# A linear attention layer with an int8 layer: x supplied transposed for the projections, and the running state updated head by head

## The chip, the cores and the metric

The kernel runs on 1 core of one Trainium2 chip. The number that counts is the device time of one launch in microseconds (us); less is better. An engine is named by its short form in the profile: PE (TensorE, matmuls), PEld (its weight loads), DVE (VectorE), ACT (ScalarE), POOL (GpSimd) and SP (SyncE, which here only issues transfers).

## The reference

Input x has the shape (8, 1024, 512), eight sequences of 1024 rows. There are 16 heads of 32 columns.

```python
x = x + attn(layernorm(x)); x = x + ffn(layernorm(x))      # layernorm: (x - mean) / sqrt(var + 1e-5)

def attn(x, qkv_w, qkv_b, out_w, out_b):
    q, k, v = split(x @ qkv_w.T + qkv_b)                    # (b, head, l, 32) each
    q = relu(q) + 1e-6;  k = relu(k) + 1e-6
    kv = cumsum(einsum('bhld,bhle->bhlde', k, v), axis=2)   # causal sum of k v^T
    k_cum = cumsum(k, axis=2)
    num = einsum('bhld,bhlde->bhle', q, kv)
    den = maximum(einsum('bhld,bhld->bhl', q, k_cum), 1e-6)
    return (num / den) @ out_w.T + out_b

def ffn(x, weight_int8, weight_scale, bias):
    x_scale = maximum(abs(x).max() / 127, 1e-5)             # one maximum over all of x
    x_int8 = clip(round(x / x_scale), -128, 127)
    return (x_int8 @ weight_int8.T) * x_scale * weight_scale.T + bias
```

The maximum over all rows splits the work in two: no row of the second layer can be scaled before the last row of the first is done.

## The kernel before

**Tiles and stages.** The rows are cut into N = 64 chunks of 128 (CB = 8 to a sequence), and two chunks are a group. The first stage (the attention) goes through the chunks in order; the second (the int8 layer) runs over 64 tiles after it. Nearly every product is made of three in float16: a value is split into a high and a low half, and high by high, high by low and low by high are added up in PSUM.

**What a chunk costs in the first stage.** DVE takes the mean and variance of its rows from xs (ln_moments), POOL refines 1/sqrt (refine_rstd), DVE writes the normalised rows xn (ln_normalise, L1578), PE turns them by four products with a float32 identity (transpose_x, L720), ACT and DVE split what comes out of PSUM into xt_hi and xt_lo (split_x, L1145 and L1589). From these PE makes q and k of a group with 8 units of 12 products (project_qk, L737) and v of a chunk with 12 (project_v, L750). The halves of q and k are moved by SP into stack, so that one product with 96 rows gives a head's scores (scores, L786); ACT copies the high half of the scores (L1201), DVE makes the low half (L1612), POOL masks both (mask, L523 and L525). PE multiplies them with v in outputs (L849 to L854), and adds the product of q with the state of all chunks before (L840). POOL also adds the bias of the output to xs (L484) and makes the low halves of q and k (L506) and of v (L515).

**The state.** A head's state is a 32 by 33 matrix (32 columns of v and a column of ones for the denominator). The keys are turned (transpose_keys, L770), and keys_values (L874) multiplies 128 key columns, which are four heads, by the 132 columns of the same four heads of v. Of the 128 by 132 result only the four blocks on the diagonal belong to a head; the rest is worked out and thrown away. For four such sets of heads in three terms that is 12 products, in two calls of six, since 4 times 132 numbers don't fit into one bank of PSUM. DVE adds each half to state (L1732), POOL multiplies state by a mask of ones and zeros (mask_state, L539), ACT and POOL split that into s_hi and s_lo (L546). The last chunk of a sequence has no update, so there are 56.

**Order.** Each engine has its own list of calls, written out by hand: a start, a loop body of one group, and an end. An engine works strictly in the order of its list, and semaphores tie the lists together. UNITS is the order in which the results of transpose_x, transpose_keys, project_qk and project_v take turns in the two banks of unit.

## Time and profile before

| | us |
|---|---|
| median of 3 runs | 1075.56 (1075.49 to 1076.29) |
| the profiled execution: its time | 1075.05 |
| the profiled execution: its span in the trace | 1073.3 |
| PE busy | 1047.6 (98%) |
| POOL busy | 866.1 (81%) |
| DVE busy | 806.8 (75%) |
| ACT busy | 727.8 (68%) |

The span runs from the first to the last instruction in the trace; the time of the execution is 1.75 us longer. "Busy" is the time in which at least one instruction of that engine was running. A matmul's duration runs until its last result is out, while the next one starts long before, so what a matmul costs PE in a dense stretch is the distance from its start to the next start and not its duration. The cost of an instruction on another engine is its duration.

### The profile page before, as it was taken

Reading aid. Unit: us, or ns where it says so; the run is one execution under the profiler, and the core shown is the slowest. Engines: PE = TensorE matmul, PEld = TensorE weight load, DVE = VectorE, ACT = ScalarE, POOL = GpSimd, SP = SyncE. Lnnn points to the kernel's source line nnn. Section 1 sums busy time; section 2 is a strip of 40 time slices with the busy share of each in tenths; the row PEclk is TensorE's granted clock in tenths of the full one; section 3 lists DMA queues with packets and bytes.
Section 4 is the critical chain, followed back from the end, with each engine's and each line's share of the span. In section 5 each row is a group of like instructions: output and inputs, shape, how many; then the busy total and the mean of one; then the engine's idle time right before and its main releaser. Section 6 shows DMA issues by size and latency. Waiting matters only on the chain.

```text
span 1073.3 us, 29299 instructions
## 1 busy us (share of the span) xinstructions
PE 1047.6 (98%) x10735; PEld 779.6 (73%) x10735; DVE 806.8 (75%) x1603; ACT 727.8 (68%) x1319; POOL 866.1 (81%) x1094
## 2 busy tenths in 40 slices
PE   5999999999999999999999999999999999998998
PEld 3777777778778777777787877877777777764554
DVE  5867777778787778777777777777777777698776
ACT  6776666676676666666766766666667667654997
POOL 2579887878788888888788887888788888893998
PEclk9999999999999999999999999999999999999999
DMA  7323343333333333333333333333333333233995
GB/s 274 80 50 93 97 109 94 86 81 91 92 90 90 86 92 97 100 88 88 91 87 87 88 92 90 87 100 99 90 87 81 90 91 93 51 117 103 383 403 211
DMA packets 74976, 120.69 MB, mean 112 GB/s; under 512 B 16465, under 2 KB 16977, under 8 KB 74834
## 3 DMA queue, kind: packets, MB, share of 16 engines
q1 hardware_dynamic: 74304, 118.29, 37.6%
q8 instruction: 86, 1.41, 0.6%
q10 hardware_dynamic: 530, 0.54, 0.2%
q14 instruction: 56, 0.46, 0.1%
HBM read 36.97 MB, written 31.46 MB: 64 GB/s over the span
## 4 chain that ended last, share of the span: by engine, by line
PE 93%; DVE 3%; ACT 1%; issue 1%; DMA 1%; POOL 1%; SPq 0%; DVEq 0%; ACTq 0%; POOLq 0%
PE unit L737 30%; PE unit L750 15%; PE misc L818 14%; PE acc L2188 5%; PE sc L786 5%; PE o_st L874 4%; PE o_st L840 3%; PE o_st L849 3%; PE unit L720 3%; PE misc L804 2%; PE unit L770 2%; PE o_st L854 2%; PE tp L2178 1%; PE acc L2193 1%; DMA stack<-qkv_wt 1%
## 5 line engine op out<-in xcount | busy, mean ns | idle before, releaser
L737 PE MATMUL unit<-xt_hi,w_hi 128*128 128x256 f16 x1000 | 273.0, 273 | 2.4 <-ACT relu L1159 2.2
L737 PE MATMUL unit<-xt_hi,w_lo 128*128 128x256 f16 x1000 | 272.9, 273 | 0.0
L737 PE MATMUL unit<-xt_lo,w_hi 128*128 128x256 f16 x1000 | 272.9, 273 | 0.0
L1159 ACT ACTIVATE relu<-unit,qk_bias_scaled 128x256 f32<-128x256 f32 x250 | 117.5, 471 | 152.1 <-PE unit L737 151.6
L1612 DVE SCALAR_TENSOR_TENSOR x_ring<-sc,x_ring 128x512 f16<-128x512 f32 x256 | 174.3, 684 | 46.8 <-ACT x_ring L1201 44.0
L506 POOL TENSOR_TENSOR qk_lo<-f_t,qk_hi 128x512 f16<-128x512 f32 x128 | 148.4, 1160 | 56.1 <-ACT qk_hi L1178 56.1
L1201 ACT ACTIVATE x_ring<-sc 128x512 f16<-128x512 f32 x256 | 148.0, 591 | 59.0 <-PE sc L786 59.0
L523 POOL TENSOR_SCALAR_AFFINE_SELECT x_ring<-x_ring 128x512 f16<-128x512 f16 x256 | 164.3, 642 | 26.4 <-DVE x_ring L1612 26.1
L525 POOL TENSOR_SCALAR_AFFINE_SELECT x_ring<-x_ring 128x512 f16<-128x512 f16 x256 | 168.0, 656 | 0.0
L737 PEld LDWEIGHTS unit<-xt_hi,w_hi 128*128 128x128 f16 x1000 | 97.8, 98 | 20.7 <-ACT relu L1159 3.0
L737 PEld LDWEIGHTS unit<-xt_lo,w_hi 128*128 128x128 f16 x1000 | 97.9, 98 | 16.4
L737 PEld LDWEIGHTS unit<-xt_hi,w_lo 128*128 128x128 f16 x1000 | 97.9, 98 | 11.6
L539 POOL TENSOR_TENSOR s_own<-state,own_head 128x528 f32<-128x528 f32 x56 | 75.2, 1343 | 28.3 <-DVE state L1732 17.5
L750 PE MATMUL unit<-w_hi,xt_hi 128*128 128x512 f16 x256 | 97.1, 379 | 0.0
L750 PE MATMUL unit<-w_hi,xt_lo 128*128 128x512 f16 x256 | 96.9, 379 | 0.0
L750 PE MATMUL unit<-w_lo,xt_hi 128*128 128x512 f16 x256 | 96.9, 379 | 0.0
L818 PE MATMUL misc<-wo_hi,at_hi 128*128 128x512 f16 x248 | 94.0, 379 | 1.6 <-DVE at_lo L1620 1.5
L786 PE MATMUL sc<-stack 96*128 96x128 f16 x1024 | 93.5, 219 | 0.8 <-DVE x_ring L1612 0.7
L818 PE MATMUL misc<-wo_hi,at_lo 128*128 128x512 f16 x248 | 94.0, 379 | 0.0
L818 PE MATMUL misc<-wo_lo,at_hi 128*128 128x512 f16 x248 | 94.0, 379 | 0.0
L1177 ACT ACTIVATE f_t<-relu,eps_scaled 128x512 f32<-128x512 f32 x128 | 92.0, 719 | 0.9 <-PE o_st L854 0.4
L546 POOL TENSOR_TENSOR s_lo<-s_own,s_hi 128x528 f16<-128x528 f32 x56 | 69.8, 1246 | 27.4 <-ACT s_hi L1222 27.4
(224 smaller groups left out, 2711.0 us busy)
## 6 DMA issues: line engine op xcount, KB each, us to landing
stack<-qk_hi SPq DMA_DIRECT2D x504, 64.0 KB, 2.0
xs<-x SPq DMA_DIRECT2D x64, 256.0 KB, 2.7
stack<-qk_lo SPq DMA_DIRECT2D x256, 64.0 KB, 2.0
out<-res SPq DMA_DIRECT2D x64, 256.0 KB, 5.3
x_spill<-xs SPq DMA_DIRECT2D x56, 256.0 KB, 2.3
x_ring<-x_spill SPq DMA_DIRECT2D x56, 256.0 KB, 5.6
stack<-qkv_wt SPq DMA_DIRECT2D x6, 512.0 KB, 8.2
x_ring<-out_wt SPq DMA_DIRECT2D x1, 1024.0 KB, 12.1
```

The lines of the kernel that those rows point to most:

```text
L506: pool.tensor_tensor(qk_lo[:, g % 2, own, :], f_t[:, own, :], qk_hi[:, g % 2, own, :], ALU.subtract).then_inc(qk_lo_done, 1)
L523: pool.affine_select(out=am_hi[:, c % 2, r, :, :], in_=am_hi[:, c % 2, r, :, :], compare_op=ALU.is_ge, fill=0.0, base=0, pattern=[[0, HG], ...
L525: pool.affine_select(out=am_lo[:, c % 2, r, :, :], in_=am_lo[:, c % 2, r, :, :], compare_op=ALU.is_ge, fill=0.0, base=0, pattern=[[0, HG], ...
L539: pool.tensor_tensor(s_own[:, :, :, :], state[:, :, :, :], own_head[:, :, :, :], ALU.mult).then_inc(s_masked, 1)
L737: mm = pe.matmul(dst[:, 0:GT], wp[:, k, f:f + P], xp[:, g % 2, k, :], start=(n == 0), stop=(n == len(terms) - 1))
L750: mm = pe.matmul(dst, xp[:, g % 2, k, j * P:(j + 1) * P], wp[:, k, 2 * E:3 * E], start=(n == 0), stop=(n == len(terms) - 1))
L786: mm = pe.matmul(sc[:, r % 2, n, :], stack[0:3 * D, par, 0, h, at], stack[0:3 * D, par, 1, h, at], start=True, stop=True)
L818: mm = pe.matmul(out_bank(c), xp[:, k, :], wp[:, k, :], start=(n == 0), stop=(n == len(terms) - 1))
L1159: act.activation(relu[:, i % 4, :], src[:, 0:GT], ACT.Relu, bias=qk_bias_scaled[:, f:f + 1]).then_inc(qk_done, 1)
L1177: act.activation(f_t[:, own, :], relu[:, at, :], ACT.Identity, bias=eps_scaled[:, side:side + 1]).then_inc(qk_eps_done, 1)
L1201: act.activation(am_hi[:, c % 2, r, :, :], sc[:, r % 2, :, :], ACT.Copy, scale=SCORE_FACTOR).then_inc(sc_copied, 1)
L1612: dve.scalar_tensor_tensor(out=am_lo[:, c % 2, r, :, :], in0=sc[:, r % 2, :, :], scalar=SCORE_FACTOR, in1=am_hi[:, c % 2, r, :, :], op0=AL ...
```

## The change

Three things change, and the lists of all engines are written anew for them.

**x supplied turned.** The kernel gets x a second time, with rows and columns of each sequence swapped (x_turned). For the chunks from 4 on, PE no longer turns anything: SP loads a group of turned rows into x_tr (load_turned). The mean and 1/sqrt of a row are now needed along the free dimension and on every partition, so they are written to memory (store_ln, 512 single numbers) and read back spread over all partitions (spread_ln) into ln_of. DVE subtracts the one and multiplies by the other in place (centre_x and scale_x), then ACT and DVE split as before, with the source in SBUF instead of PSUM. The statistics are taken from a further copy of the rows, xa (load_rows), up to eight groups ahead, so x is read three times. The first four chunks go the old way.

**The state head by head.** keys_values is one call of 32 products. A product takes the 32 key columns of one head and writes to the 32 partitions of PSUM that are this head's. With the high half of the keys it multiplies the high and the low half of v at once, 66 columns, and with the low half of the keys the high half of v, 33 columns. state shrinks from 528 to 264 numbers on a partition, in two parts that POOL adds (s_sum) ahead of the mask. DVE adds to state once per chunk and not twice.

**Buffers and semaphores.** x_tr and xa take the place at the start of x1_ring where weights were staged; the staging of out_wt goes to xs, and the last four of the first eight chunks are loaded into xs later. Semaphores are merged.

```diff
-wo_stage = spare[:, 0:EC * E].rearrange("p (c n) -> p c n", c=EC)
+x_tr = spare[:, 0:4 * E].rearrange("p (s k t) -> p s k t", s=2, k=EC)
+xa = spare[:, 4 * E:8 * E].rearrange("p (s c e) -> p s c e", s=2, c=GROUP)
+wo_stage = xs[:, AHEAD:CB, :]
...
-state = buf(one, "state", [P, HG, 4, VW])
-own_head = buf(one, "own_head", [P, HG, 4, VW])
+state = buf(one, "state", [P, HG, 2, VW])
+s_sum = buf(one, "s_sum", [P, HG, VW])
+own_head = buf(one, "own_head", [P, 4, VW])
...
-UNITS = (("v", 1), ("xt", 1), ("kt", 1), ("qk", 0), ("qk", 1),
-         ("qk", 2), ("qk", 3), ("qk", 4), ("qk", 5), ("qk", 6),
-         ("kt", 0), ("qk", 7), ("xt", 0), ("v", 0))
+UNITS = (("kt", 1), ("v", 1), ("qk", 3), ("qk", 4), ("kt", 0),
+         ("qk", 5), ("qk", 6), ("qk", 7), ("v", 0), ("qk", 0),
+         ("qk", 1), ("qk", 2))
...
+    def load_rows(g, since=3):
+        if not since <= g < N // GROUP:
+            return
+        if g >= 4:
+            sp.wait_ge(ln_stats, upto(GROUP * (g - 2) + 1))
+        if g == 2:
+            sp.wait_ge(bias_squared, 1)
+            sp.wait_ge(sums_ready, 3)
+        sp.dma_start(xa[:, g % 2, :, :], x_pairs[g]).then_inc(xa_loaded[g % 2], 16)
+    def load_turned(g, since=3):
+        if not since <= g < N // GROUP:
+            return
+        if g >= 4:
+            sp.wait_ge(xt_lo_done, upto(GROUP * (g - 2) + 1))
+        sp.dma_start(x_tr[:, g % 2, :, :], x_turned_of[g]).then_inc(turned_loaded[g % 2], 16)
...
+    def store_ln(g, since=3):
+        if not since <= g < N // GROUP:
+            return
+        sp.wait_ge(ln_step, (g + 1) * LN_STEPS)
+        sp.dma_start(ln_rows[g].rearrange("k c p -> p (k c)"), mrv[:, g % 2, 0:2, :].rearrange("p k c -> p (k c)"),
+                     allow_slow_non_contiguous=True).then_inc(ln_stored[g % 2], 16)
+    def spread_ln(g, since=3):
+        if not since <= g < N // GROUP:
+            return
+        sp.wait_ge(ln_stored[g % 2], g // 2 * 16)
+        if g >= 4:
+            sp.wait_ge(xt_ready, upto(GROUP * (g - 2) + 1))
+        sp.dma_start(ln_of[:, g % 2, :, :].rearrange("p k t -> p (k t)"),
+                     ln_rows[g].rearrange("k c p -> (k c p)").partition_broadcast(P)).then_inc(turned_loaded[g % 2], 16)
...
-    for n in range(6, N - 2, GROUP):
+    for n in range(8, N - 2, GROUP):
         g = n // GROUP
+        load_rows(g + 8)
+        store_x1(n - 5)
+        load_next_x(n - 8)
...
-        pool.wait_ge(s_added, 2 * updates(c) + 2)
+        pool.wait_ge(s_added, updates(c) + 1)
         if updates(c) > 0:
             pool.wait_ge(s_lo_done, updates(c))
-        pool.tensor_tensor(s_own[:, :, :, :], state[:, :, :, :], own_head[:, :, :, :], ALU.mult).then_inc(s_masked, 1)
+        pool.tensor_tensor(s_sum[:, :, :], state[:, :, 0, :], state[:, :, 1, :], ALU.add).then_inc(s_summed, 1)
+        pool.wait_ge(s_summed, updates(c) + 1)
+        pool.tensor_tensor(s_own[:, :, :, :], s_sum[:, :, :].unsqueeze(2).to_broadcast([P, HG, 4, VW]), own_head[:, :, :].unsqueeze(1).to_broadcast([P, HG, 4, VW]), ALU.mult).then_inc(s_masked, 1)
...
-    def keys_values(c, half):
+    def keys_values(c):
         if not updates_state(c):
             return
         par, _at = place(c)
-        if half == 0:
-            pe.wait_ge(kn_done, updates(c) + 1)
-            pe.wait_ge(v_lo_done, upto(c))
-        if 2 * updates(c) + half > 0:
-            pe.wait_ge(s_added, 2 * updates(c) + half)
-        terms = ((0, v_hi), (0, v_lo), (1, v_hi))
-        for i in range(2):
-            g = 2 * half + i
-            for n, (kp, vp) in enumerate(terms):
-                mm = pe.matmul(st[:, i * 4 * VW:(i + 1) * 4 * VW].rearrange("p (h w) -> p h w", w=VW), kn[:, kp, g, :],
-                               vp[:, par, c % GROUP, 4 * g:4 * g + 4, :],
-                               start=(i == 0 and n == 0), stop=(i == 1 and n == len(terms) - 1), skip_group_check=True)
+        pe.wait_ge(kn_done, updates(c) + 1)
+        pe.wait_ge(v_lo_done, upto(c))
+        if updates(c) > 0:
+            pe.wait_ge(s_added, updates(c))
+        for g in range(HG):
+            for a in range(4):
+                pe.matmul(st[a * D:(a + 1) * D, 2 * g * VW:2 * (g + 1) * VW].rearrange("p (s w) -> p s w", w=VW),
+                          kn[:, 0, g, a * D:(a + 1) * D], v_halves[:, par, c % GROUP, 4 * g + a, :, :],
+                          start=(g == 0), stop=False, skip_group_check=True)
+            for a in range(4):
+                mm = pe.matmul(st[a * D:(a + 1) * D, (2 * g + 1) * VW:2 * (g + 1) * VW], kn[:, 1, g, a * D:(a + 1) * D],
+                               v_hi[:, par, c % GROUP, 4 * g + a, :], start=False, stop=(g == HG - 1), skip_group_check=True)
...
-        project_v(g, 1)
-        transpose_attn(n - 3)
-        scores(n - 1, 2)
-        keys_values(n - 2, 1)
...
+        outputs(n, 1)
+        transpose_keys(n + 1)
+        scores(n + 1, 3)
+        project_v(g + 2, 1)
+        scores(n + 2, 0)
+        project_out(n - 1)
+        project_qk(g + 2, 3)
+        keys_values(n + 1)
...
-        if src is None:
-            src = unit[:, unit_bank[("xt", c % GROUP)], :]
-        if c >= AHEAD:
+        if c < AHEAD:
+            src = (unit[:, unit_bank[("xt", c % GROUP)], :] if src is None else src).rearrange("p (c n) -> p c n", c=EC)
+        else:
+            src = x_tr[:, c // GROUP % 2, :, c % GROUP * P:(c % GROUP + 1) * P]
             act.wait_ge(qk_ready, (c // GROUP - 1) * QK)
             act.wait_ge(v_ready, upto(GROUP * (c // GROUP) - 3))
         act.wait_ge(xt_ready, upto(c))
         act.activation(xt_hi[:, c // GROUP % 2, :, c % GROUP * P:(c % GROUP + 1) * P],
-                       src.rearrange("p (c n) -> p c n", c=EC), ACT.Copy).then_inc(xt_hi_done, 1)
+                       src, ACT.Copy).then_inc(xt_hi_done, 1)
...
+        if g >= 4:
+            dve.wait_ge(ln_stored[g % 2], (g - 2) // 2 * 16)
+        if g >= 2:
+            dve.wait_ge(xa_loaded[g % 2], g // 2 * 16)
         for c in (GROUP * g, GROUP * g + 1):
-            dve.wait_ge(x_loaded[c % CB], (c // CB + 1) * 16)
-            dve.bn_stats(stats[:, c % GROUP, :], xs[:, c % CB, :]).then_inc(ln_stats, 1)
+            if g < 2:
+                dve.wait_ge(x_loaded[c], 16)
+            rows = xs[:, c, :] if g < 2 else xa[:, g % 2, c % GROUP, :]
+            dve.bn_stats(stats[:, c % GROUP, :], rows).then_inc(ln_stats, 1)
         for c in (GROUP * g, GROUP * g + 1):
             dve.wait_ge(ln_stats, upto(c))
             dve.nop(nofuse=True)
-            dve.bn_aggr(mv[:, c % GROUP, :], stats[:, c % GROUP, :]).then_inc(ln_mv, 1)
+            dve.bn_aggr(mrv[:, g % 2, 0:3:2, c % GROUP], stats[:, c % GROUP, :]).then_inc(ln_mv, 1)
         dve.wait_ge(ln_mv, upto(GROUP * g + 1))
-        dve.tensor_scalar(ve[:, :], mv[:, :, 1], LN_EPS, None, ALU.add).then_inc(ln_var, 1)
+        dve.tensor_scalar(ve[:, :], mrv[:, g % 2, 2, :], LN_EPS, None, ALU.add).then_inc(ln_var, 1)
...
+    def turned(c):
+        return x_tr[:, c // GROUP % 2, :, c % GROUP * P:(c % GROUP + 1) * P]
+    def spread(c, kind):
+        return ln_of[:, c // GROUP % 2, kind, c % GROUP * P:(c % GROUP + 1) * P].unsqueeze(1).to_broadcast([P, EC, P])
+    def centre_x(c, since=AHEAD):
+        if not since <= c < N:
+            return
+        g = c // GROUP
+        dve.wait_ge(turned_loaded[g % 2], g // 2 * 32)
+        dve.tensor_tensor(turned(c), turned(c), spread(c, 0), ALU.subtract).then_inc(x_centred, 1)
+    def scale_x(c, since=AHEAD):
+        if not since <= c < N:
+            return
+        dve.wait_ge(x_centred, upto(c - AHEAD))
+        dve.tensor_tensor(turned(c), turned(c), spread(c, 1), ALU.mult).then_inc(xt_ready, 1)
...
-    def add_to_state(c, half):
+    def add_to_state(c):
         if not updates_state(c):
             return
-        dve.wait_ge(st_ready, 2 * updates(c) + half + 1)
+        dve.wait_ge(st_ready, updates(c) + 1)
         if updates(c) > 0:
             dve.wait_ge(s_masked, updates(c))
-        own = state[:, 2 * half:2 * half + 2, :, :].rearrange("p g h w -> p (g h w)")
-        new = st[:, 0:8 * VW]
+        own = state[:, :, :, :].rearrange("p g s w -> p (g s w)")
+        new = st[:, 0:2 * HG * VW]
...
+        "x_turned": np.swapaxes(L0_attn_x, 1, 2),
```

In the loop of PE, transpose_x is gone and keys_values stands once. What the names mean: L720 turns a chunk, L874 updates half of the state, L786 are scores, L737 and L750 are projections. In the middle of the program PE had this order:

```order
L737 MATMUL unit<-xt_hi,w_lo 128x256
L720 MATMUL unit<-ident,xn 128x128 x4
L874 MATMUL o_st<-v_halves,kn 128x132 x6
L786 MATMUL sc<-stack 128x128 x4
L750 MATMUL unit<-w_hi,xt_hi 128x512
```

In the changed kernel the place of an update, between two projections, reads:

```order
L834 MATMUL unit<-xt_hi,w_lo 128x256
L971 MATMUL o_st<-v_halves,kn 32x66 x4
L975 MATMUL o_st<-v_halves,kn 32x33 x4
L971 MATMUL o_st<-v_halves,kn 32x66 x4
L975 MATMUL o_st<-v_halves,kn 32x33 x4
L971 MATMUL o_st<-v_halves,kn 32x66 x4
L975 MATMUL o_st<-v_halves,kn 32x33 x4
L971 MATMUL o_st<-v_halves,kn 32x66 x4
L975 MATMUL o_st<-v_halves,kn 32x33 x4
L850 MATMUL unit<-w_hi,xt_hi 128x512
```

The four turning products are gone, and two times six products of 132 columns have become 16 of 66 and 16 of 33.

On DVE, the statistics (L1553), the normalising (L1578) and the low half of xt (L1589) of a group stood like this in the loop, with L1612 the low half of scores and L1705 to L1716 the division:

```order
L1553 BN_STATS stats<-xs 128x6 x2
L1557 BN_AGGR mv<-stats 128x2 x2
L1559 TENSOR_SCALAR ve<-mv 128x2
L1612 SCALAR_TENSOR_TENSOR x_ring<-sc,x_ring 128x512
L1566 RECIPROCAL r<-sq 128x2
L1578 TENSOR_SCALAR xn<-xs,mv,rstd 128x512 x2
L1612 SCALAR_TENSOR_TENSOR x_ring<-sc,x_ring 128x512
L1705 TENSOR_SCALAR den<-o_st,den_eps 128x16
L1708 RECIPROCAL rden<-den 128x16
L1710 TENSOR_TENSOR o_st<-o_st,num 128x2x7x32
L1716 TENSOR_TENSOR attn<-o_st,rden 128x512
L1589 TENSOR_TENSOR xt_lo<-unit,xt_hi 128x4x128
```

In the changed kernel L1707 subtracts the mean (x_ring with ln_of is x_tr), L1714 scales, L1749 is the low half of scores, L1740 adds the bias of v and L1842 to L1853 are the division:

```order
L1749 SCALAR_TENSOR_TENSOR x_ring<-sc,x_ring 128x512
L1707 TENSOR_TENSOR x_ring<-x_ring,ln_of 128x4x128
L1757 TENSOR_TENSOR at_lo<-misc,at_hi 128x512
L1749 SCALAR_TENSOR_TENSOR x_ring<-sc,x_ring 128x512
L1842 TENSOR_SCALAR den<-o_st,den_eps 128x16
L1845 RECIPROCAL rden<-den 128x16
L1847 TENSOR_TENSOR o_st<-o_st,num 128x2x7x32
L1853 TENSOR_TENSOR attn<-o_st,rden 128x512
L1740 TENSOR_TENSOR v<-unit,v_bias 128x16x32
L1714 TENSOR_TENSOR x_ring<-x_ring,ln_of 128x4x128 x2
L1749 SCALAR_TENSOR_TENSOR x_ring<-sc,x_ring 128x512
```

Where a chunk had one instruction with one tile as its source, it now has two, each with two sources in SBUF, and the scaling of both chunks of a group stands in a row.

## Rows read from the trace of the kernel before

**Rows 1.** The page: busy time and share of the span, by engine.
```profile
PE 1047.6 (98%) x10735; PEld 779.6 (73%) x10735; DVE 806.8 (75%) x1603; ACT 727.8 (68%) x1319; POOL 866.1 (81%) x1094
```
**Rows 2.** Windows: length, busy us per engine with instructions, clock, DMA share, GB/s.
```profile
core 0: us, PE busy (x) PEld busy (x) DVE busy (x) ACT busy (x) POOL busy (x), PEclk, DMA share, GB/s
0.00:60.00 60.00, 46.81 (x364) 32.46 (x365) 41.73 (x87) 42.29 (x71) 26.96 (x48) 0.97 0.53 169
...
100.00:935.00 835.00, 834.93 (x8951) 644.67 (x8948) 631.72 (x1232) 556.62 (x1038) 688.77 (x893) 1.00 0.33 89
...
1000.00:1073.00 73.00, 69.09 (x474) 37.05 (x472) 51.66 (x106) 66.44 (x103) 68.58 (x54) 1.00 0.88 329
```
**Rows 3.** Windows for line L804 alone, four products per chunk, same stretch.
```profile
100.00:935.00 835.00, 33.80 (x224) 25.70 (x224) 1.00 0.33 89
```
**Rows 4.** Waits of PE: who waited for whom, us in total, times, longest.
```profile
PE o_st L885 <- ACT x_ring L1266: 12.0, 2, 9.0
PE unit L818 <- DVE at_lo L1620: 2.5, 2, 1.4
PE unit L737 <- ACT relu L1159: 2.2, 2, 1.5
```
**Rows 5.** Timeline of PE: start us, duration us, then the instruction.
```profile
502.26 0.53 PE L874 MATMUL o_st<-v_halves,kn 128*128 128x132 f16 x6
502.62 0.60 PE L720 MATMUL unit<-ident,xn 128*128 128x128 f32 x4
503.06 0.39 PE L786 MATMUL sc<-stack 96*128 96x128 f16 x4
...
503.64 0.19 PE L849 MATMUL o_st<-v_halves,x_ring 128*128 128x66 f16 x1
503.67 0.18 PE L854 MATMUL o_st<-v_halves,x_ring 128*128 128x33 f16 x1
503.69 0.19 PE L849 MATMUL o_st<-v_halves,x_ring 128*128 128x66 f16 x1
503.73 0.18 PE L854 MATMUL o_st<-v_halves,x_ring 128*128 128x33 f16 x1
503.75 0.19 PE L849 MATMUL o_st<-v_halves,x_ring 128*128 128x66 f16 x1
```
**Rows 6.** Groups of DVE instructions: busy us, mean ns, idle before and its releaser.
```profile
L1578 DVE TENSOR_SCALAR xn<-xs,mv,rstd 128x512 f32<-128x512 f32 x64 | 50.5, 828 | 34.7 <-POOL rstd L498 34.7
L1589 DVE TENSOR_TENSOR xt_lo<-unit,xt_hi 128x512 f16<-128x512 f32 x62 | 42.2, 682 | 6.9 <-ACT xt_hi L1145 6.9
L1732 DVE SCALAR_TENSOR_TENSOR state<-o_st,state 128x264 f32<-128x264 f32 x96 | 41.0, 427 | 18.3 <-PE o_st L874 17.7 <-POOL s_own L539 0.5
L1837 DVE TENSOR_SCALAR x_ring<-w_safe 128x512 f32<-128x512 f32 x1 | 0.4, 417 | 0.0
L1839 DVE TENSOR_TENSOR w_safe<-w_safe,x_ring 128x512 f32<-128x512 f32 x1 | 0.7, 681 | 0.0
```
**Rows 7.** Groups of POOL instructions.
```profile
L539 POOL TENSOR_TENSOR s_own<-state,own_head 128x528 f32<-128x528 f32 x56 | 75.2, 1343 | 28.3 <-DVE state L1732 17.5 <-DVE state L1730 10.9
L493 POOL TENSOR_TENSOR t<-t,ve 128x2 f32<-128x2 f32 x32 | 6.3, 196 | 2.5
```
**Rows 8.** Line L539: duration ns min/median/max, first and last start.
```profile
L539 POOL TENSOR_TENSOR s_own<-state,own_head x56: 1298/1307/3281, 60.7 to 960.9; 128x528 f32<-128x528 f32 x56
```
**Rows 9.** Timeline of DVE, two stretches.
```profile
60.43 2.34 DVE L1825 SCALAR_TENSOR_TENSOR wo_lo<-x_ring,wo_scale,wo_hi 128x2048 f16<-128x2048 f32 x1
...
492.84 1.60 DVE L1578 TENSOR_SCALAR xn<-xs,mv,rstd 128x512 f32<-128x512 f32 x2 [1.22 <-POOL rstd L498]
```
**Rows 10.** Timeline of POOL, the same two stretches.
```profile
60.66 3.28 POOL L539 TENSOR_TENSOR s_own<-state,own_head 128x528 f32<-128x528 f32 x1 [0.71 <-DVE state L1730]
...
492.75 0.64 POOL L523 TENSOR_SCALAR_AFFINE_SELECT x_ring<-x_ring 128x512 f16<-128x512 f16 x1
493.34 0.81 POOL L525 TENSOR_SCALAR_AFFINE_SELECT x_ring<-x_ring 128x512 f16<-128x512 f16 x1
```
**Rows 11.** The page: DMA queue, packets, MB, share of 16 engines' span.
```profile
q1 hardware_dynamic: 74304, 118.29, 37.6%
```
**Rows 12.** The page: DMA issues, KB each, median us from issue to landing.
```profile
xs<-x SPq DMA_DIRECT2D x64, 256.0 KB, 2.7
```

More of the change, by code:

```diff
@@ new lines, in _ @@
+                scores(5, 3)
+                outputs(4, 1)
+                keys_values(5)
+                project_out(3)
+                project_v(4, 1)
+                project_qk(4, 3)
+                scores(6, 0)
+                scores(6, 1)
+                outputs(5, 0)
+                outputs(5, 1)
+                transpose_attn(4)
+                scores(6, 2)
+                project_qk(4, 4)
+                transpose_keys(6)
+                project_qk(4, 5)
+                project_out(4)
@@ new lines, in _ @@
+                project_qk(4, 6)
+                project_qk(4, 7)
+                project_v(5, 0)
+                scores(6, 3)
+                keys_values(6)
+                scores(7, 0)
+                project_qk(5, 0)
+                outputs(6, 0)
+                scores(7, 1)
+                transpose_attn(5)
+                project_qk(5, 1)
+                project_qk(5, 2)
+                scores(7, 2)
+                outputs(6, 1)
+                project_v(5, 1)
+                project_out(5)
@@ new lines, in _ @@
+                scores(7, 3)
+                scores(8, 0)
+                project_qk(5, 3)
+                project_qk(5, 4)
+                scores(8, 1)
+                transpose_attn(6)
+                outputs(7, 0)
+                outputs(7, 1)
+                scores(8, 2)
+                project_out(6)
+                scores(8, 3)
+                transpose_keys(8)
+                project_qk(5, 5)
+                project_qk(5, 6)
+                project_qk(5, 7)
+                project_v(6, 0)
@@ L1440, in _ @@
+                ln_root(7)
                 split_attn(3)
[L1442 to L1455 removed]
+                features(4, 0)
@@ L1456, in _ @@
+                features(5, 0)
+                features(5, 1)
+                features(5, 2)
+                copy_low(6)
+                copy_scores(7, 2)
+                copy_scores(7, 3)
+                split_state(6)
+                split_x(12)
+                split_x(13)
+                copy_scores(8, 0)
+                split_values(9)
+                for n in range(8, N - 2, GROUP):
+                    g = n // GROUP
                     copy_scores(n, 1)
                     split_attn(n - 2)
+                    features(g + 1, 3)
+                    split_values(n + 2)
```

1112 lines of the change are left out of this document (557 added, 555 removed).

## Prediction

> **What bounds the kernel now.** I read four views, from coarse to fine. The page's first part shows PE busy for 98% of the span and POOL next with 81% [rows 1]. That average mixes stages, so the windows come second: from 100 to 935 us PE is busy 834.93 of 835 us, POOL 688.77, DVE 631.72 and ACT 556.62, at full clock [rows 2]. PE works on four turning products of L804 per chunk, and there are 224 in the window [rows 3], so it holds 56 chunks and a chunk lasts 835 / 56 = 14.91 us. Third, the waits of PE: after the 12 us for squares of the weights at the start, its two longest sums are 2.5 and 2.2 us [rows 4]. So in the first stage the time is the sum of what PE is given to do, and nothing else is late. In the last 73 us ACT and POOL are busy for 66 and 69 us and the DMA engines for 88% [rows 2]; the second stage is not touched. Work taken from PE in the first stage is a gain until another engine becomes the bound: per chunk POOL has 14.91 - 688.77 / 56 = 14.91 - 12.30 = 2.61 us to spare, DVE 3.63, ACT 4.97.
>
> **The turning products go.** The fourth view is PE's timeline. Four products of L720 start at 502.62 us and the next line at 503.06 [rows 5]: 0.44 us a chunk. 60 of the 64 chunks lose them, 60 x 0.44 = 26.4 us, and since no time of PE is idle there, all of it lies on the path. What replaces them runs on SP, DVE and ACT. ACT does what it did.
>
> **The state update on PE.** Six products of 132 columns take 502.62 - 502.26 = 0.36 us [rows 5], so a chunk's two calls take 0.72. The trace has no product that uses part of the array's columns, so I bound it. A pair of 66 and 33 columns takes (503.75 - 503.64) / 2 = 0.055 us in outputs [rows 5]. If the 16 pairs of a chunk go one behind another, 16 x 0.055 = 0.88 us. If the four products that write to four different strips of partitions run side by side, 4 x 0.055 = 0.22 us. If besides PE has to empty before the first and after the last of them, there is the part of a product that others now cover: L854 lasts 0.18 us and the next starts 0.03 later, so 0.15 us twice, and 0.88 + 0.30 = 1.18 us. I take 0.75, near the row of single pairs, with a little overlap: +0.03 x 56 = +1.7 us. The ends are -0.50 x 56 = -28 and +0.46 x 56 = +26 us.
>
> The Trainium skill ("TensorEngine Tiling (Array Packing)", Key Properties) says that tiles of the array can load weights and multiply in parallel, and that a change of tiling mode drains the engine. The first would give about the -28 end, the second the drain of the +26 end; no row here shows either, since every product of before has 128 columns of weights.
>
> **DVE.** A chunk loses the normalising, 0.83 us, and one of two additions to the state, 0.43 x 7/8 = 0.37 [rows 6]. It gains centre_x and scale_x: 512 float32 numbers from two tiles in SBUF took 0.68 us at L1839 [rows 6], so 1.36 us. split_x keeps its 0.68. The sum is 11.28 + 1.36 - 1.20 = 11.44 us of about 14.5, and fits.
>
> **POOL.** The new addition has 132 columns; between 0.20 us for 2 columns [rows 7] and 1.31 for 528 [rows 8] it comes to 0.20 + 130 / 526 x 1.11 = 0.47 us, or 0.41 per chunk. The multiplication keeps its 528 columns. That alone gives 12.71 us.
>
> But POOL and DVE hold each other up, and this is the term to weigh. L1825 reads two tiles in SBUF from 60.43 to 62.77 us [rows 9]; L539 starts on POOL at 60.66 and takes 3.28 us [rows 10] where its median is 1.31 [rows 8]. It loses 1.97 us and so stands still until 62.63, 0.14 before DVE is done. An instruction of 0.68 us with two sources in SBUF thus costs a POOL that has work up to 0.54 us. The other way round, L1578 takes 0.83 us on average beside a busy POOL and the same kind 0.42 without one (L1837) [rows 6], and the select that comes up during it takes 0.81 instead of 0.64 [rows 9, 10]. The change makes three DVE instructions per chunk of this sort: centre_x, scale_x, and split_x, whose source moves from PSUM to SBUF. It takes away one L1578. POOL: 12.71 + 3 x 0.54 - 0.17 = 14.16 us per chunk. DVE: 0.4 us of waiting for each of the three, as L1578 had, 11.44 + 1.2 = 12.6.
>
> The Trainium skill ("SBUF — State Buffer", Who interferes with whom) states that a VectorE instruction with two SBUF inputs contends with a GpSimd instruction that reads SBUF, and that the second to issue fully blocks. Rows 9 and 10 agree for the case in which DVE is first, POOL loses 1.97 of the 2.11 us from its start to DVE's end; that DVE waits with two plain sources when POOL is first, no row of before shows.
>
> PE would now need 14.91 - 0.44 + 0.03 x 7/8 = 14.50 us per chunk, POOL 14.16. The room of POOL falls from 2.61 to 0.34 us. Both keep their lists' order, so a delayed select or qk_lo will now and then reach PE through scores or outputs. I charge 4 us for the stage, 0.07 per chunk, between nothing and the rival below.
>
> **Transfers.** Each group of two chunks adds 512 single numbers, 512 packets of x_turned, 256 of rows and 128 of the spread, 1408 packets. A packet took 0.376 x 16 x 1073.3 / 74304 = 0.087 us of one engine [rows 11], so 1408 x 0.087 / 16 = 7.7 us in 29, 26% on top of the 33% of the stage [rows 2]. These are four DMAs more per group in SP's queue, between stack transfers. But SP's loop issues the rows for the statistics (g + 8) one group, 29 us, before DVE's loop reads them (g + 7), and the turned rows and the spread (g + 4) two groups before centre_x (g + 2). A load of 256 KB lands in 2.7 us [rows 12]. PE waits for no DMA now. I charge nothing; if the cover were gone, each group would pay up to 2.7 us.
>
> **Start and end.** The first 60 us hold 13 us of idle PE [rows 2], nearly all for the squares [rows 4]. The lists there are reordered, with three sums of squares ahead of the first projection instead of two. I take 0, with 3 us either way.
>
> **Sum.** 1075.05 - 26.4 + 1.7 + 4 = 1054.4 for an execution like the profiled one. That one was 0.5 us under the median of the runs, so I forecast 1055 us, its own range 1045 to 1066.
>
> **Rivals.** *The strips run side by side.* For it: four products in a row go to four different strips. PE would then need 14.91 - 0.44 - 0.44 = 14.03 us and POOL's 14.16 is the bound; with 0.2 us of idle it gives 14.36, and 56 x 0.55 = 31 us less, 1044; if POOL is held up less than I think, down to 1075.6 - 26.4 - 28 = 1021. I put the case at 1038.
>
> *Each update empties the array twice.* 1075.6 - 26.4 + 26 = 1075, plus up to 4 us of waits: 1075 to 1079, no gain. For it: 0.15 us of every small product is now hidden by the next. Against it: the order puts each update between long projections, whose weights are loaded ahead.
>
> *POOL becomes the bound: slower than before.* Of POOL's 2.61 us of idle time per chunk, part is waiting for ACT and DVE, which its work does not shorten. If half of it, 1.3 us, stays on top of 14.16, a chunk takes 15.46 and the stage 0.55 x 56 = 31 us more, 1106. It decides from 14.91 - 14.16 = 0.75 us of idle POOL per chunk. For it: rows 9 and 10, and that the two scalings and the two splits stand in pairs, between which POOL can take the port again. Against it: much of that idle time is there because PE is slow today.
>
> *The numbers of LayerNorm come late.* The mean and 1/sqrt go out as single numbers and back over all partitions, and SP waits for each step in its own order, with stack transfers behind. If that wait took the place of the products removed, the gain of 26 us would be eaten: 1080 or more. Against it: SP stores group g + 6, spreads g + 4 and DVE centres g + 2 in the same turn of the loop, so each step has two groups, 58 us.
>
> **How the numbers follow.** Forecast 0.42; strips side by side 0.22; array emptied 0.14; POOL as the bound 0.18; LayerNorm late 0.04. A change under 0.2%, 2.2 us, can't be told from none. Faster: 0.42 + 0.22 + 0.05 of the third = 0.69. Same: 0.05 of the third. Slower: 0.04 of the third, 0.18 and 0.04 = 0.26. The range runs from 1032, which holds most of the second case, to 1084, which holds the third and leaves out most of the fourth.
>
> **What will show it.** The windows from 100 to 900 us with 56 chunks: a period near 14.6, PE still above 97% busy, POOL above 93%. In PE's timeline, 32 products of the update within 0.75 us: 0.25 would mean side by side, 1.2 with gaps at both ends the emptying. centre_x and scale_x at 0.68 us alone and about 1.1 on average, and POOL's selects at L615 more often above 0.64. The waits of PE with sums of several us on DVE's low scores or POOL's masks. The forecast is wrong if PE's waits sum to over 15 us, or if a DMA stands in them.

## The result and the profile after

The kernel after takes 1105.07 us (median of 3 runs, 1104.89 to 1110.37) against 1075.56: a ratio of 1.029, 95% interval 1.024 to 1.034. It is slower; 1055 was forecast. Its profiled execution was the longest of the three, 1110.37 us. Its trace spans 1108.6 us, 35.3 more than before, so what follows accounts for these 35.3 us and not for the 29.5 between the medians.

The page's first lines (busy us by engine, then PE's clock in tenths over 40 slices and the DMA queue), against [rows 1] and [rows 11]:

```profile
PE 1030.3 (93%) x11615; PEld 731.3 (66%) x11615; DVE 856.0 (77%) x1607; ACT 727.7 (66%) x1319; POOL 922.1 (83%) x1150
...
PEclk9999898999999999999999999999999999979999
...
q1 hardware_dynamic: 118464, 157.68, 50.3%
```

PE is busy for 17 us less and stands still for 53 us more. The windows say where (the columns of [rows 2]; the last one answers to its third):

```profile
0.00:60.00 60.00, 40.42 (x222) 23.64 (x223) 34.15 (x78) 33.09 (x54) 21.45 (x41) 0.94 0.61 189
60.00:200.00 140.00, 114.17 (x1294) 82.95 (x1293) 88.09 (x165) 72.17 (x139) 99.83 (x135) 0.93 0.55 112
200.00:930.00 730.00, 714.82 (x8654) 527.33 (x8652) 602.43 (x1085) 495.68 (x920) 650.90 (x820) 1.00 0.48 132
1035.00:1108.00 73.00, 69.34 (x475) 37.17 (x473) 51.73 (x107) 66.69 (x103) 68.76 (x54) 1.00 0.88 331
```

From 200 us on PE is busy for 98%; before that it stands still for 45 of 200 us, and the clock falls to 0.93. The kernel before has, behind its first window [rows 2],

```profile
60.00:200.00 140.00, 138.33 (x1493) 107.88 (x1491) 101.14 (x198) 95.32 (x177) 118.16 (x152) 1.00 0.32 86
```

and stands still for 15 of the 200 us. To follow the loss I take the start of the last turning product of attention of a chunk, in the traces (for chunk 8 it is the last of these four, before and after):

```profile
186.65 0.61 PE L804 MATMUL misc<-ident,attn 128*128 128x128 f32 x4
```
```profile
233.29 0.61 PE L904 MATMUL misc<-ident,attn 128*128 128x128 f32 x4
```

The table gives how many us later than in the kernel before that start comes, for the kernel after and for the experiments below; the last column is the time from chunk 8 to chunk 58, over 50 (14.85 us before).

```
                            chunk 0     4     8    32    58    63   us per chunk
after                          15.8  41.6  46.6  40.9  26.6  35.2   14.45
e1 state update alone           0.5   0.4  -0.4  -6.3 -13.0 -11.2   14.60
e2 no store                     6.7  14.2  13.3   2.6 -14.4  -6.7   14.30
e3 store on ACT's queue        35.3  56.4  72.9  78.6  84.2  92.4   15.08
e4 one source                  18.7  45.8  51.6  47.5  36.3  45.4   14.54
e5 rows of 32                   9.3  17.4  15.0   3.1 -13.0  -5.7   14.29
e6 128 single numbers          12.8  28.9  28.2  21.2   5.4  13.3   14.40
e7 no store, no loads           7.0  13.9  10.5   0.3 -15.2  -7.6   14.34
e8 no store, one source         6.7  12.5  11.7   0.6 -16.2  -6.6   14.29
e9 no wait at the spread       16.7  39.2  37.5  31.3  18.0  26.0   14.46
e10 stores from group 10 on     6.9  15.0  18.3  10.9  -0.5   7.4   14.47
```

So the 35 us are +46.6 in the first eight chunks, -20.0 in the next fifty and +8.6 in the last five. The steady stretch did what I forecast (14.57 us per chunk), and a little more.

PE's waits after, against [rows 4], where none named a DMA (who waited for whom, us in total, times, longest):

```profile
PE sc L886 <- DMA stack<-qk_lo: 16.6, 3, 6.9
PE sc L886 <- issue: 12.8, 15, 2.1
PE unit L834 <- ACT relu L1253: 9.8, 5, 6.5
PE o_st L985 <- ACT x_ring L1360: 9.0, 3, 8.0
```

and of SP's:

```profile
SPq L391 <- DMA ln_rows<-mrv: 18.4, 4, 6.5
```

The scores now wait for transfers. What SP does at the first such wait, in its timeline:

```profile
37.55 1.86 SPq L447 DMA_DIRECT2D stack<-qk_lo  x3
39.46 0.59 SPq L380 DMA_DIRECT2D ln_rows<-mrv  x1
40.09 0.54 SPq L373 DMA_DIRECT2D x_ring<-x_turned  x1
41.06 2.43 SPq L447 DMA_DIRECT2D stack<-qk_lo  x4
```

and how the chain of waits goes on from there, and at 82 us (start, duration, what):

```profile
42.90 12.17 DMA stack<-qk_lo
55.07 0.14 issue
55.20 1.01 PE sc L886 x8
...
82.27 10.27 DMA ln_rows<-mrv
92.56 0.34 SPq L391
```

A stack transfer lands in 2.0 us at the median. This one took 12.17; the store of LayerNorm's single numbers (L380) had been issued 3.4 us ahead of it, and behind the store a load of turned rows (L373), which e5 below has in the same place. The store of 82.27 took 10.27 us to land, and SP stood at the spread (L391) for the end of it. The waits name the store only at L391; what it does to the transfers behind it shows as their landing.

It does it to transfers of another queue too. ACT issues eight stack transfers of its own (stack<-qk_hi, L1400) from 37.6 us on, in its own queue. Here are the last five of them, issued behind SP's store of 39.46, in the kernel after, and the same five in e5, which stores the same numbers as rows (count, duration of the issue in ns, starts; then us from issue to landing):

```profile
L1400 ACTq DMA_DIRECT2D stack<-qk_hi x5: 546/612/828, 39.7 to 42.5; - x5
DMA to landing us min/median/max: 9.2/11.7/11.8
```
```profile
L1401 ACTq DMA_DIRECT2D stack<-qk_hi x5: 612/617/815, 39.9 to 42.5; - x5
DMA to landing us min/median/max: 2.1/4.1/4.3
```

So the delay is not in SP's queue alone: it lies where the transfers of both queues pass.

### The profile page after: what moved, and what is told of

It reads as the page before. It is cut to its first block, busy times and chain, and to the rows that moved or that the text cites. A ratio compares the mean times of both kernels' runs of the same rounds, so it can differ in the third digit from the quotient of the medians.

```text
span 1108.6 us, 31189 instructions
## 1 busy us (share of the span) xinstructions
PE 1030.3 (93%) x11615; PEld 731.3 (66%) x11615; DVE 856.0 (77%) x1607; ACT 727.7 (66%) x1319; POOL 922.1 (83%) x1150
## 4 chain that ended last, share of the span: by engine, by line
PE 77%; DMA 7%; DVE 6%; issue 3%; ACT 3%; SPq 2%; POOL 1%; another core or an unknown queue 0%; ACTq 0%; DVEq 0%; POOLq 0%
PE unit L834 24%; PE unit L850 13%; PE misc L918 13%; PE sc L886 5%; PE acc L2340 5%; PE o_st L940 3%; DMA ln_rows<-mrv 3%; PE o_st L949 3%; PE misc L904 2%; PE unit L870 2%; SPq L447 2%; PE o_st L954 1%; PE tp L2330 1%; DMA stack<-qk_lo 1%; PE acc L2345 1%
## 5 line engine op out<-in xcount | busy, mean ns | idle before, releaser
L613 POOL TENSOR_SCALAR_AFFINE_SELECT x_ring<-x_ring 128x512 f16<-128x512 f16 x256 | 177.9, 695 | 28.5 <-DVE x_ring L1749 28.2
L1749 DVE SCALAR_TENSOR_TENSOR x_ring<-sc,x_ring 128x512 f16<-128x512 f32 x256 | 172.7, 683 | 27.2 <-ACT x_ring L1295 26.8
L596 POOL TENSOR_TENSOR qk_lo<-f_t,qk_hi 128x512 f16<-128x512 f32 x128 | 152.7, 1207 | 32.7 <-ACT qk_hi L1272 31.8
L615 POOL TENSOR_SCALAR_AFFINE_SELECT x_ring<-x_ring 128x512 f16<-128x512 f16 x256 | 176.1, 688 | 0.0
L886 PE MATMUL sc<-stack 96*128 96x128 f16 x1024 | 94.0, 222 | 37.2 <-DMA stack<-qk_lo 16.6
L886 PEld LDWEIGHTS sc<-stack 96*128 96x128 f16 x1024 | 68.8, 98 | 68.0 <-issue 33.1
L638 POOL TENSOR_TENSOR s_lo<-s_own,s_hi 128x528 f16<-128x528 f32 x56 | 67.5, 1206 | 52.1 <-ACT s_hi L1316 52.1
```

The source lines that it names most:

```text
L596: pool.tensor_tensor(qk_lo[:, g % 2, own, :], f_t[:, own, :], qk_hi[:, g % 2, own, :], ALU.subtract).then_inc(qk_lo_done, 1)
L613: pool.affine_select(out=am_hi[:, c % 2, r, :, :], in_=am_hi[:, c % 2, r, :, :], compare_op=ALU.is_ge, fill=0.0, base=0, pattern=[[0, HG], ...
L615: pool.affine_select(out=am_lo[:, c % 2, r, :, :], in_=am_lo[:, c % 2, r, :, :], compare_op=ALU.is_ge, fill=0.0, base=0, pattern=[[0, HG], ...
L638: pool.tensor_tensor(s_lo[:, c % 2], s_own[:, :, :, :], s_hi[:, c % 2], ALU.subtract).then_inc(s_lo_done, 1)
L886: mm = pe.matmul(sc[:, r % 2, n, :], stack[0:3 * D, par, 0, h, at], stack[0:3 * D, par, 1, h, at], start=True, stop=True)
L1749: dve.scalar_tensor_tensor(out=am_lo[:, c % 2, r, :, :], in0=sc[:, r % 2, :, :], scalar=SCORE_FACTOR, in1=am_hi[:, c % 2, r, :, :], op0=AL ...
```

## The experiments

Twelve kernels ran. The kernel before, timed again beside them, took 1075.96 us (for e1 to e4), 1075.75 (e5 to e8) and 1075.14 (e9 to e12); each ratio is against the one of its own set. "Price" is the time above e2, the kernel without the store.

**e1, the state update alone.** In the kernel before, the six products of 132 columns in each of two calls become 32 products of one head each in one call, with POOL's addition:

```diff
-state = buf(one, "state", [P, HG, 4, VW])
+state = buf(one, "state", [P, HG, 2, VW])
+s_sum = buf(one, "s_sum", [P, HG, VW])
```

> The kernel before with the state update alone taken from the change: 32 products of one head each in one call at the place of the first of the two calls, the halved state, POOL's added sum; x is turned on PE as before, and every list keeps its order. From the changed kernel's trace the 32 products take about 0.3 us against 0.72. If PE stays the bound, 56 x 0.42 = 23.5 us less: about 1052. If the strips cost a wait around each update after all, or POOL's extra 0.4 us per chunk reaches PE, over 1060. If this part is what made the changed kernel slow, over 1076.

1063.51 us, ratio 0.988 (0.987 to 0.990), where 1052 was expected if PE stayed the bound, and over 1060 if the strips cost a wait or POOL's addition reached PE: half of the change is a gain by itself, 12.4 us, and the fastest kernel of all. PE's timeline in the kernel after shows the price (start, duration):

```profile
507.87 0.27 PE L834 MATMUL unit<-xt_hi,w_lo 128*128 128x256 f16 x1
508.07 0.21 PE L971 MATMUL o_st<-v_halves,kn 128*32 128x66 f16 x4
508.11 0.19 PE L975 MATMUL o_st<-v_halves,kn 128*32 128x33 f16 x4
...
508.29 0.19 PE L975 MATMUL o_st<-v_halves,kn 128*32 128x33 f16 x4
508.40 0.39 PE L850 MATMUL unit<-w_hi,xt_hi 128*128 128x512 f16 x1
```

Products of four strips start as one group, and eight groups start within 0.22 us. From 507.87 to 508.40 are 0.53 us, of which the product ahead takes 0.11 itself (the spacing in its series): 0.42 us a chunk, against 0.72 before. Within it the first group comes 0.20 us after the product ahead, 0.09 more than its own 0.11, and the product behind 0.11 after the last group. Between "side by side" (0.22) and "emptied twice" (1.18) it is the first with a part of the second. The gain of 0.30 x 56 = 17 us shrinks to 12.4; what takes the rest no run shows.

**e2, no store.** Of the kernel after, with the waits for it:

```diff
-sp.dma_start(ln_rows[g]..., mrv[:, g % 2, 0:2, :]...)
-sp.wait_ge(ln_stored[g % 2], g // 2 * 16)
-    ln_rows[g].rearrange("k c p -> (k c p)").partition_broadcast(P)
+    out_b.partition_broadcast(P)
```

> The changed kernel without the store of the mean and 1/sqrt as 512 single numbers: SP still waits for the numbers, then spreads a fixed row of the same size (out_b) in place of them, so the rows it normalises with are not the right ones. Queue theory (the store lies 7 to 14 us in SP's one queue with bulk loads ahead and stack transfers behind it, and SP stands at the spread until it has landed): the loss of the first 200 us goes, 1105 - 35 = about 1070, and the steady stretch gets shorter too, down to 1055. Port theory (DVE's instructions with two sources in SBUF and POOL hold each other up): under 8 us less, 1097 to 1105.

1070.78 us, ratio 0.996 (0.994 to 0.997), 34 less than the kernel after. Queue theory holds (about 1070), though nothing of its further gain down to 1055; port theory (1097 to 1105) is out. At chunk 8 it is 13.3 us late instead of 46.6, and it gains 0.55 us per chunk instead of 0.40. One store in 29 us, of 2 KB, is the loss. (e2 also drops the waits for the store; e9 and e5 below separate the two.)

**e3, the store on ACT's queue**, issued behind the next group's square root:

```diff
-sp.dma_start(ln_rows[g]...)
+act.wait_ge(ln_step, (g + 1) * LN_STEPS)
+act.dma_start(ln_rows[g]...)
```

> The changed kernel with that store issued by ACT into its own queue, one group later than before on SP's list, right after the root of the next group; nothing left out. Queue theory: stack transfers no longer lie behind the store, but the spread still waits for it: 1070 to 1090. Port theory: no change, 1100 to 1110.

1168.89 us, ratio 1.087 (1.085 to 1.090). All expectations missed. The store now comes a group later, and DVE waits for what it feeds:

```profile
DVE x_ring L1716 <- DMA ln_of<-ln_rows: 29.5, 2, 17.6
DVE stats L1676 <- DMA ln_rows<-mrv: 12.0, 1, 12.0
```

This run can't tell the queue from what lies behind it, since it moved the store in time too. The landings of ACT's transfers in the section above can.

**e4, one source.** DVE's centring, scaling and low half are left out, and in their place stand instructions that read one source and write one number (the first of three is shown):

```diff
-dve.tensor_tensor(turned(c), turned(c), spread(c, 0), ALU.subtract)
+dve.tensor_reduce(scrap[:, 0, c:c + 1], turned(c), AX.XY, ALU.max)
```

> The changed kernel with DVE's centring, scaling and low half of x replaced (chunks from 4 on) by a maximum over the same tile, which reads one source in SBUF and takes as long alone (0.65 to 0.69 us): what is left out is the normalising of x and its low half. Port theory: DVE's waits of 0.2 to 0.4 us at each and POOL's longer selects go; the steady stretch falls from 14.4 to about 14.1 us per chunk, 56 x 0.3 = 17 us, 1088, and if the start is held up by POOL too, 1075. Queue theory: the start keeps its loss, over 1090.

1119.79 us, ratio 1.040 (1.037 to 1.042), over the 1090 of queue theory and far from port theory's 1088: slower still, though POOL's busy time fell from 922.1 to 870.0 us and DVE's from 856.0 to 812.8. POOL's selects show what they were held up by, 643 ns instead of 688 (busy us, mean ns, idle time ahead):

```profile
L616 POOL TENSOR_SCALAR_AFFINE_SELECT x_ring<-x_ring 128x512 f16<-128x512 f16 x256 | 164.6, 643 | 0.0
```
```profile
L615 POOL TENSOR_SCALAR_AFFINE_SELECT x_ring<-x_ring 128x512 f16<-128x512 f16 x256 | 176.1, 688 | 0.0
```

The contention is real. That it is not what makes the kernel late, e8 shows. Why it got 15 us slower I did not settle.

**e5, rows of 32.** DVE turns the numbers in blocks of 32 x 32 (mrv is widened to 32 columns), and the store writes 16 rows of 128 bytes; the result is that of the kernel after. In the loop the store stands one group later in SP's list (g + 5 instead of g + 6), since the turning comes between:

```diff
+dve.transpose(mrt[:, g % 2, :], mrv[:, g % 2, :, :].rearrange("p k c -> p (k c)"))
-sp.dma_start(ln_rows[g]..., mrv[:, g % 2, 0:2, :]...)
+for q in range(4):
+    sp.dma_start(ln_rows[g].rearrange("k c p -> (k c) p")[:, q * 32:(q + 1) * 32],
+                 mrt[q * 32:q * 32 + 4, g % 2, :])
```

> The kernel after with LayerNorm's numbers stored as rows: DVE turns each block of 32 x 32 numbers (one more small instruction per two chunks), so that the 512 single numbers become 16 rows of 32 numbers, in four DMAs of four rows. Everything else of the change stays, the result too. Theory (the landing of 512 single numbers holds SP's queue and through it the stack transfers and the spread): the store then lands like other small transfers, nothing stands behind it, and the time comes to that of the kernel without the store, 1070.8 us, within 4 us: 1067 to 1075. Rival (what costs is that the numbers go through DRAM and back at all, a write's completion of several us whatever its count of rows): 1095 to 1110.

1071.75 us, ratio 0.997 (0.996 to 0.998): as without a store, and faster than the kernel after by 33 us and than the kernel before by 4. In SP's timeline the same place as above is

```profile
39.57 1.66 SPq L382 DMA_DIRECT2D ln_rows<-mrt  x4
41.28 0.53 SPq L374 DMA_DIRECT2D x_ring<-x_turned  x1
41.86 2.46 SPq L449 DMA_DIRECT2D stack<-qk_lo  x4
```

and PE starts the scores at 53.68 from DVE's work, with no DMA in the chain:

```profile
52.34 0.69 DVE v L1751
53.03 0.61 DVE x_ring L1760
...
53.68 0.40 PE sc L887 x4
```

**e6, 128 single numbers** instead of 512:

```diff
-sp.dma_start(ln_rows[g]..., mrv[:, g % 2, 0:2, :]...)
+sp.dma_start(ln_rows[g, 0, 0], mrv[:, g % 2, 0, 0:1])
```

> The kernel after with a quarter of the store: only the means of the first chunk of a group go out, 128 single numbers instead of 512, and the spread reads one bias vector in their place, so LayerNorm's numbers are wrong; all waits stay. Theory (the price is per single number): between the kernel without the store, 1070.8, and the kernel after, 1105, near a quarter of the way: 1076 to 1085. Rival (a price per store, whatever its size): over 1095.

1090.32 us, ratio 1.015 (1.011 to 1.019): a quarter of the numbers costs more than half of the price. Neither expectation holds as it stands.

**e7, no store and no loads** from group 4 on: load_rows, load_turned and spread_ln return at once there.

> The kernel without the store (1070.8 us), and also without the transfers that replace the turning, from group 4 on: rows for the statistics, turned rows, spread. DVE works on what lies there, so the numbers of x are wrong. Theory A (the bulk loads cost through the queue: the start loses 13 us and the end 8 by stack transfers that stand behind them): the start loss shrinks to 7 or less and the time falls to 1050 to 1060. Theory B (the loss at start and end lies in the order of the lists and in DVE's and POOL's longer instructions): within 3 us of 1070.8.

1066.62 us, ratio 0.991 (0.990 to 0.993). 4 us less: 84 transfers of 256 to 512 KB cost almost nothing. Theory A (1050 to 1060, and 7 us or less lost at the start) is out, since 10.5 us are still lost by chunk 8; theory B's 3 us are missed by 1.2. Most of what is left is not the queue.

**e8, no store and one source**, e2 with the edit of e4:

> The kernel without the store, in which DVE's centring, scaling and low half of x (from chunk 4 on) are replaced by a maximum over the same numbers that reads one source and writes one number, so that DVE holds the port less; the numbers of x are wrong. Theory (what is left of the loss is DVE and POOL holding each other up): below 1065, with the steady stretch gaining about 0.7 us per chunk against the kernel before instead of 0.55. Rival (the port is not on the path): within 3 us of 1070.8.

1067.24 us, ratio 0.992 (0.990 to 0.994). 3.5 us less, between the theory (below 1065) and its rival (within 3 us of 1070.8), and 14.29 us per chunk as in e2 (14.30): the port costs at most 3 or 4 us here. Where, the traces don't show: the profiled executions of e2 and e8 took the same, 1068.32 and 1068.48 us.

**e9, no wait at the spread**, the store stays:

```diff
-sp.wait_ge(ln_stored[g % 2], g // 2 * 16)
```

> The kernel after with the store of 512 single numbers as it is, but SP does not wait for it at the spread, which reads one bias vector instead, so LayerNorm's numbers are wrong; only DVE still waits for a store two groups old before it writes over its source. Theory A (what costs is that SP stands at the spread until the store has landed, with everything behind it in its list): near the kernel without the store, 1070.8 us, at most 1078. Theory B (the store holds up the transfers that are issued behind it, whether SP waits or not): over 1088, and the stack transfers behind a store still take 8 us and more. I hold B, since 10 us went by in the trace between a store's issue and the landing of a load behind it.

1102.18 us, ratio 1.025 (1.023 to 1.026). Theory B (over 1088) holds: SP's standing at the spread is worth 3 us of the 34. (By the table it would be 9, but there the kernel after stands with its longest execution.) The scores wait as before for what was issued behind the store:

```profile
PE sc L885 <- DMA stack<-qk_lo: 16.4, 3, 7.3
```

**e10, stores from group 10 on.**

```diff
-if not since <= g < N // GROUP:
+if not 10 <= g < N // GROUP:
```

> The kernel after with the stores of single numbers from group 10 on only, as in the loop; the first eight are left out, and all spreads read one bias vector, so LayerNorm's numbers are wrong. Theory (in the steady loop the store hides: there after gained 0.4 us per chunk with the store and 0.55 without it; the price is paid in the first eight chunks, where five stores stand among transfers that PE waits for): 1071 plus about 0.15 x 40 = 6 at most, 1071 to 1079. Rival (each store costs about the same anywhere): 22 of 30 stores are left, so 1071 + 34 x 22 / 30 = 1096.

1083.55 us (1077.38 to 1085.42), ratio 1.007 (1.005 to 1.009). Theory (1071 to 1079) and rival (1096) were both missed. 22 of 30 stores cost 12.8 of the 34 us, 0.6 each; the first eight cost 21.5, 2.7 each. The place decides, but the loop doesn't hide them: 14.47 us per chunk against 14.30 without.

**e11, 16 single numbers.**

```diff
-sp.dma_start(ln_rows[g]..., mrv[:, g % 2, 0:2, :]...)
+sp.dma_start(ln_rows[g, 0, 0, 0:16], mrv[0:16, g % 2, 0, 0:1])
```

> The kernel after with a store of 16 single numbers in place of 512, the spread reading one bias vector, so LayerNorm's numbers are wrong; all waits stay. 512 numbers cost 34 us of time, 128 cost 19.5, 16 rows of 128 bytes cost 1. Theory A (the number of single writes sets the price): 1071 to 1074. Theory B (a write of 4 bytes lands late however few there are): 1085 to 1092, as with 128.

1069.93 us, ratio 0.994 (0.993 to 0.996): no price. Theory B (1085 to 1092) is out.

**e12, 128 rows of 4 numbers**, all 512 numbers in 128 writes of 16 bytes:

```diff
-sp.dma_start(ln_rows[g].rearrange("k c p -> p (k c)"), mrv...)
+sp.dma_start(ln_rows[g].rearrange("k c p -> (k c p)").rearrange("(p f) -> p f", f=4), mrv...)
```

> The kernel after with the store as 128 rows of 4 numbers, one for each partition, all 512 numbers in 128 writes of 16 bytes; the spread reads one bias vector, so LayerNorm's numbers are wrong; all waits stay. Theory A (the number of writes sets the price): as the kernel that stores 128 single numbers, 1090, within 4 us. Theory B (the size of a write sets it, and 16 bytes are easier than 4): 1071 to 1082.

1069.06 us, ratio 0.995 (0.994 to 0.997): no price, and theory A (1090) is out. e6 and e12 send the same number of packets; the pages' lines on the queue and on the store (KB each, median us to landing) read, for e6,

```profile
q1 hardware_dynamic: 106944, 157.64, 51.3%
ln_rows<-mrv SPq DMA_DIRECT2D x30, 0.5 KB, 10.2
```

and for e12

```profile
q1 hardware_dynamic: 106944, 157.68, 50.2%
ln_rows<-mrv SPq DMA_DIRECT2D x30, 2.0 KB, 6.5
```

Four times the bytes land 3.7 us sooner and the kernel is 21 us faster. Together:

| store of a group | writes x bytes | us |
|---|---|---|
| none (e2) | | 1070.8 |
| e11 | 16 x 4 | 1069.9 |
| e5 | 16 x 128 | 1071.8 |
| e12 | 128 x 16 | 1069.1 |
| e6 | 128 x 4 | 1090.3 |
| after | 512 x 4 | 1105.1 |

Many writes of 4 bytes are what costs; neither their number alone (e12) nor their size alone (e11). One rival stands untested: e6 puts its 128 numbers side by side in memory, so 16 of its writes fall on 64 bytes where e12 has 4. Whether the size of a write or the crowding of writes on one place sets the price would take a store of 128 single numbers spread apart.

## Why the prediction was wrong

**The step that failed is "Transfers".** I priced the single numbers by the mean packet of the queue, 0.087 us of one engine, and by the room in their due times, and charged nothing. The share itself came out smaller than I worked out: from 200 to 930 us the DMA engines' share is 0.48 for 0.33 before, 0.15 more, where I had 0.26. A single number takes far less of it than a mean packet: by the pages of the kernel after and of e12, which stores as many bytes in a quarter of the writes, 11520 packets more go with 348 us more, 0.03 us each and not 0.087. So the price was not in the share. 512 writes of 4 bytes landed after 10.27 us, and transfers issued behind them, whose due times were not two groups off, landed with them: the stack transfers, which PE waits for. I had looked at how early LayerNorm's numbers were stored and not at who stands behind them in SP's list at the start. e2, e5 and e9 show it: 34 us come back without the store, 33 with the store as rows, and only 3 without SP's wait.

The rival *The numbers of LayerNorm come late*, to which I gave 0.04, had the place right ("stack transfers behind") and part of the mechanism wrong: it counted on SP's wait. Its "each step has two groups" holds in the loop; in the first eight chunks the lists issue stores among the stack transfers. And in the loop, where the steps do have their two groups, the stores still cost 0.6 us each (e10).

**Start and end (0, 3 us either way)** was wrong as well. With the store as rows e5 takes 1071.75 us, still 17 over the forecast of 1055. Without the store chunk 8 is still 13 us late, and the last five chunks lose 7 to 10 in all kernels with the new lists. At the start e7 gives back 3 of them and e8 2; the rest I can only place. In e5 PE stands still for 22.3 us of the first 200 (windows, 46.28 + 131.41 busy), 7.5 more than before. At the end, as I read the lists (no run tests it), the last projections come late and nothing stands between them and the scores that need them. In e5's chain:

```profile
926.43 1.50 PE unit L835 x12
...
930.32 0.62 ACT qk_hi L1273
...
934.74 2.04 DMA stack<-qk_hi
...
938.19 1.99 DMA stack<-qk_lo
940.27 0.58 PE sc L887 x4
```

12 us from the projection to the scores, which in the loop lie beside the next group's projections.

**The clock** followed from both and I had not counted it. It is granted at 0.93 in the first 200 us, 0.99 before. PE had stood still there for 45 us; in the same kernel with the store as rows it is 0.97. Part of the 46.6 us is thus work done at the lower of the two levels, 1.2 GHz: by my estimate at most 0.06 x 200 = 12 us, the difference of the two mean clocks over that stretch.

**The turning products (-26.4).** The size fits. In the steady stretch e1 gains 0.25 us a chunk and e2 0.55, so dropping them and bringing the rest is worth 0.30 of the 0.44; in e5 PE's idle time from 200 to 930 us is 6 us, 0.12 per chunk.

**The state update (+1.7, between -28 and +26)** is a term mis-sized the other way: 0.42 us per chunk, not 0.75, so -0.30 x 56 = -17 on PE and -12.4 in e1. The row of single pairs to which I held was of products that follow one another on the same columns. Of the two statements of the Trainium skill ("TensorEngine Tiling (Array Packing)", Key Properties) the trace agrees with the first, tiles do run in parallel. A drain it shows only in part: entry and exit cost about 0.2 us together, 0.09 and 0.11, where I had 0.15 twice for an array that empties.

**DVE and POOL.** Low halves took 1060 ns and the two steps of normalising 874 and 809, I had 1.1; POOL 922.1 us in all for 866.1 before:

```profile
L1726 DVE TENSOR_TENSOR xt_lo<-x_ring,xt_hi 128x512 f16<-128x512 f32 x60 | 61.5, 1060 | 0.0
L1707 DVE TENSOR_TENSOR x_ring<-x_ring,ln_of 128x512 f32<-128x512 f32 x60 | 52.4, 874 | 18.6 <-DMA x_ring<-x_turned 10.9 <-DMA ln_of<-ln_rows 7.8
L1714 DVE TENSOR_TENSOR x_ring<-x_ring,ln_of 128x512 f32<-128x512 f32 x60 | 46.5, 809 | 0.0
```

The contention is there, as the Trainium skill ("SBUF — State Buffer", Who interferes with whom) says, and is not the bound. POOL's 56 us more are 1.0 per chunk, where I had 14.16 - 12.30 = 1.86. The rival *POOL becomes the bound* gave 1106, next to the measured time, and is refuted all the same: e5 keeps POOL as busy (921.8 us) and is 33 us faster, and e8 frees DVE's port and gains 3.5. A number that fits is no evidence for its mechanism.

**What I said would prove it wrong** came: PE's waits sum to over 15 us, and a DMA stands in them (16.6 us for stack<-qk_lo alone).

## What to carry to other kernels

Price a transfer by what is issued behind it, and by the size of its writes, not by its bytes: 2 KB in 512 writes of 4 bytes cost 34 us over 30 stores here, the same 2 KB in 16-byte or 128-byte writes nothing. One transposition by DVE ahead of the store was enough, with the right result (e5). Writing the four numbers of a partition side by side was as fast (e12), but there the spread read something else: reading numbers stored in that order back as rows was not tried.

Split a change: of this one, half was worth 12.4 us alone, and the whole lost 29.5. In a kernel with an order written out, look at the first and last chunks apart from the loop, since a cover that the loop has is missing there.

## What the runs showed of the hardware

- 128 writes of 4 bytes landed after 10.2 us at the median, 128 of 16 bytes after 6.5, 16 of 4 bytes after 6.4 (e6, e12, e11; in e6 the trace has half of the landings). Stack transfers behind 512 of them landed up to 12.17 us after issue, for 2.0 at the median of all. Transfers in ACT's queue behind a store in SP's landed as late (median 11.7 us, against 4.1 behind the store as rows), so they don't wait in SP's queue alone. Whether they wait at the DMA engines or at the memory is open.
- Products on 32 columns of the array ran four at a time, one group every 0.02 to 0.04 us for 66 or 33 columns. The first came 0.09 us later than its predecessor's own time, the product behind 0.11 us after the last group.
- In e5 PE stood still for 5.4 us from 60 to 80 us, and the granted clock was 0.83 there, 0.91 from 80 to 100 with PE busy again, and 1.00 from 100 to 120.
